# A graph stage whose edge lists are rounded to 8 columns, and whose merge and gates run by halves

## The reference

```python
h = (x_flat @ W_gat).reshape(M, HEADS, NUM_EXPERTS)       # M = 8192, 4 heads x 4 experts
src = jnp.concatenate([edge_index[0], loops]); dst = jnp.concatenate([edge_index[1], loops])
e = leaky_relu(a_src[src] + a_dst[dst], 0.2)
ee = jnp.exp(e - segment_max(e, dst)[dst])
alpha = ee / (segment_sum(ee, dst)[dst] + 1e-16)
agg = segment_sum(h[src] * alpha[:, :, None], dst).reshape(M, 16) + b_gat
scores = layernorm(agg, ln_gamma, ln_beta).reshape(M, HEADS, NUM_EXPERTS).mean(1)
topk_s, topk_i = top_k(scores, 2); w = softmax(topk_s)
# out = sum over 4 experts of gate * (gelu(x @ W1[e] + b1[e]) @ W2[e] + b2[e])
```

## Time and profile before

| what | us |
|---|---|
| median of three runs | 2720.1 |
| the profiled execution's own time | 2713.4 |
| its span, first to last instruction | 2711.6 |
| sort, stages 0 to 2, list places | 0 to 866 |
| gathers and blocks | 866 to 1567 |
| last block to first tok_end fetch | 1567 to 1579 |
| 64 fetches | 1579 to 1660 |
| merge and gates | 1660 to 1708 |
| experts of stage 3, layernorm | 1708 to 1831 |
| stages 4 to 7 | 1831 to 2712 |

### The profile page before, as it was taken

The page is one execution under the profiler, slowest core; times in us unless marked ns, Lnnn a source line. Parts: engine busy times, 40 slices in busy tenths (PEclk is TensorE's granted clock), DMA queues, the critical chain, the costliest instruction groups (busy, mean ns, idle before and its releaser), DMA issues.

```text
span 2711.6 us, 19548 instructions
## 1 busy us (share of the span) xinstructions
PE 1360.3 (50%) x6758; PEld 601.1 (22%) x6758; DVE 1406.3 (52%) x2023; ACT 634.9 (23%) x1011; POOL 813.8 (30%) x870
## 2 busy tenths in 40 slices
PE   2637421488761000000000010889977999979889
PEld 1424321322330000000000000224544222224432
DVE  7999999866634310111111114546236555566566
ACT  1301200065010000000000001543024666630043
POOL 1000000177347877777777763000000000000000
PEclk8756655599875555555555555899988999989989
DMA  9200000000134011111111100001000000000000
GB/s 394 110 1 1 0 0 0 22 14 13 27 12 69 12 20 14 20 20 14 20 20 14 20 14 5 1 1 24 0 1 4 1 1 1 1 7 0 0 1 32
DMA packets 62636, 63.00 MB, mean 23 GB/s; under 512 B 42821, under 2 KB 56533, under 8 KB 60117
## 3 DMA queue, kind: packets, MB, share of 16 engines
q1 hardware_dynamic: 36532, 52.16, 6.4%
q0 software_dynamic: 26016, 9.69, 3.5%
HBM read 21.68 MB, written 40.11 MB: 23 GB/s over the span
## 4 chain that ended last, share of the span: by engine, by line
PE 31%; POOL 28%; DVE 25%; issue 12%; ACT 1%; DMA 0%; POOLq 0%; DVEq 0%; SPq 0%; ACTq 0%
POOL rows L1766 19%; DVE keys L2029 13%; PE bank L814 9%; PE bank L505 7%; PE bank L542 7%; POOL keys L1911 5%; POOL scratch_start L1758 2%; POOL tok_end L1781 2%; PE bank L445 2%; DVE x_pair L1352 2%; PE bank L527 2%; PE bank L413 2%; DVE keys L2027 1%; PE bank L538 1%; DVE wide L451 1%
## 5 line engine op out<-in xcount | busy, mean ns | idle before, releaser
L1766 POOL DMA_INDIRECT rows<-scratch_row,idx_ring x544 | 533.2, 980 | 165.8 <-issue 165.8
L737 DVE TENSOR_TENSOR hid<-hid,bank 128x512 f32<-128x512 f32 (+1 forms) x320 | 273.0, 895 | 232.3 <-PE bank L527 231.4
L1436 PE MATMUL bank<-ident,last 128*20 128x128 f32 x3 | 0.8, 409 | 739.5 <-DVEq L1626 739.5
L2029 DVE TENSOR_TENSOR keys<-keys 128x1024 f32<-128x1024 f32 (+1 forms) x388 | 353.5, 953 | 7.3
L613 ACT ACTIVATE hid<-bank,weights_odd 128x512 f32<-128x512 f32 x448 | 281.2, 685 | 176.1 <-PE bank L505 174.4
L505 PE MATMUL bank<-wide,weights_odd 64*128 64x512 f32 x896 | 268.2, 679 | 106.0 <-ACT hid L613 105.4
L1594 DVE COPY idx_ring<-src_i 128x32 int32 (+1 forms) x17 | 3.3, 194 | 546.6 <-DMA rows<-scratch_row,idx_ring 546.4
L542 PE MATMUL bank<-hid,weights_odd 128*64 128x512 f32 x896 | 242.2, 621 | 0.5 <-DVE hid L737 0.5
L766 POOL MEMSET wide<- 128x132 f32 (+2 forms) x3 | 1.0, 333 | 748.4 <-DVEq L1053 336.8
L1911 POOL DMA_INDIRECT keys<-scratch_sorted,weights_odd x128 | 123.7, 966 | 221.4 <-DVEq L2082 179.8
L814 PE MATMUL bank<-wide,weights_even 128*128 128x512 f32 x416 | 186.4, 603 | 1.5 <-issue 1.5
(11 more groups left out here) (414 smaller groups left out, 2004.0 us busy)
## 6 DMA issues: line engine op xcount, KB each, us to landing
scratch_sums<-wide SPq DMA_DIRECT2D x12, 2048.0 KB, 35.9
rows<-scratch_row,idx_ring POOLq DMA_INDIRECT x544, 2.4
...
```

What stands on the lines that cost most here:

```text
L737: v.tensor_tensor(blocks, blocks, bank[4 + b][:, :].unsqueeze(1).broadcast_to([P, KS, 512]), ALU.mult).then_inc(S("scaled"), 1)
L1766: g.indirect_dma_start(out=rows[:, b, c, :], out_offset=None, in_=row_d[:, :], in_offset=at(idx_ring[:, b, c:c + 1])).then_inc(s_gath[b], 16)
L2029: m = v.tensor_tensor(o, p, q, op)
```

## The change

The lists' length is rounded to 8 columns (`PART`) instead of 32. Blocks that need all four parts stay in the loop; a partly filled one runs behind the loop: GpSimd gathers 8, 16 or 24 of its columns, VectorE walks all 32, and columns behind the list's end are made harmless by adding -1e30 to their `a_dst_e` (`behind_end`) and setting their `same` to 1. ScalarE and SyncE keep the old loop. The merge buffers move to another place in memory. What the merge can do without the fetched ends is done ahead; the rest runs by halves of 32 tiles: the first half and its gates ahead of the experts, the second inside VectorE's expert steps 5 to 10. ScalarE's exponentials and roots for it move among its gelus, and the next stage's layernorms of stage 3 begin at step 22 instead of 13 and follow each third step instead of each fourth.

```diff
+LATE = 5
+LN3 = [max(4 * n + 13, 3 * n + LATE + 17) for n in range(8)]
...
-        pe.wait_ge(S("s3_tok_carry"), 4)
...
-    for i in range(SPREAD_LAG, BLOCKS + LAG + 5):
+    for i in range(SPREAD_LAG, LN3[7] + 4 if st == 3 else BLOCKS + LAG + 5):
...
-        if 1 <= i - SPREAD_LAG <= 6:
-            gates_in(1 + i - SPREAD_LAG)
+        if gates_at(st, i) is not None:
+            gates_in(gates_at(st, i))
...
+        if st == 3:
+            for n in range(8):
+                if i == LN3[n] + 3:
+                    ln_back(pe, 4, n)
+            for n in range(8):
+                if i == LN3[n] + 1:
+                    ln_var(pe, 4, n)
+            for n in range(8):
+                if i == LN3[n]:
+                    ln_centre(pe, 4, n)
+        elif st != 7:
...
+    k = i - SPREAD_LAG
+    if st == 3:
+        return {1: 2, 2: 3, LATE + 7: 4, LATE + 8: 5, LATE + 9: 6, LATE + 10: 7}.get(k)
+    return 1 + k if 1 <= k <= 6 else None
...
+    for i in range(LN3[7] + 2 if st == 3 else 8 * NH + LAG + 7):
-        if i == 3:
+        if st == 3:
+            if i == SPREAD_LAG:
+                merge_exp(a, 0)
+                merge_root(a, 0)
+                gate_exp(0)
+            if i == LATE + 7:
+                merge_exp(a, 1)
+            if i == LATE + 9:
+                merge_root(a, 1)
+            if i == LATE + 11:
+                gate_exp(1)
+        if i == 3 and st != 3:
             gate_exp(0)
         if i == SPREAD_LAG:
-            gate_exp(1)
+            if st != 3:
+                gate_exp(1)
             gate_rows(0)
             gate_rows(1)
...
+        if st == 3:
+            for n in range(8):
+                if i == LN3[n] + 1:
+                    ln_root(a, 4, n)
+                if i == LN3[n]:
+                    ln_square(a, 4, n)
...
-    gate_vector(v, link, st)
+    split_gates = gate_vector(v, link, st)
+    if st == 3:
+        largest, second, shares = split_gates
+        for step in range(4):
+            merge_vector(v, link, 0, step)
+        largest(0)
+        second(0)
+        shares(0)
+    def second_half(s):
+        if LATE <= s < LATE + 4:
+            merge_vector(v, link, 1, s - LATE)
+        if s == LATE + 3:
+            largest(1)
+        if s == LATE + 4:
+            second(1)
+        if s == LATE + 5:
+            shares(1)
...
+    for s in range(LN3[7] if st == 3 else 8 * NS + 8 // KS + 1):
+        if st == 3:
+            second_half(s)
+            for n in range(8):
+                if s == LN3[n] - 5:
+                    ln_recip(v, 4, n)
+                if s == LN3[n] - 3:
+                    ln_scale(v, 4, n)
...
+def merge_exp(a, h):
+    a.wait_ge(S("s3_merge_in"), 2 + 2 * h)
+    nc.scalar.activation(wgt2[h][:, :, :, :], wgt2[h][:, :, :, :], ACT.Exp).then_inc(S("s3_merge_exp"), 1)
+def merge_root(a, h):
+    part = slice(h * HNT, (h + 1) * HNT)
+    a.wait_ge(S("s3_merge_in"), 3 + 2 * h)
+    nc.scalar.activation(sc2[:, part], sc2[:, part], ACT.Sqrt).then_inc(S("s3_merge_exp"), 1)
...
+    link(v.tensor_scalar(behind_end, col_iota, span[:, 0:1], NEG, ALU.is_ge, ALU.mult))
...
+    link(v.scalar_tensor_tensor(same[:, :], col_iota, span[:, 0:1], same[:, :], ALU.is_ge, ALU.max))
...
-    link(v.tensor_scalar(limits, list_w, float(WIN * P), None, ALU.mult))
-    link(v.memset(limits[:, 0:2], -1.0))
+    for q in range(4):
+        link(v.tensor_scalar(limits[:, q, :], list_w, float(WIN * P), float(q * PART * P), ALU.mult, ALU.add))
+    link(v.memset(limits[:, :, 0:2], -1.0))
     link(v.tensor_scalar(limits, limits, total, None, ALU.is_lt))
-    link(v.tensor_reduce(span[:, 1:2], limits, AX, ALU.add))
-    link(v.tensor_reduce(span[:, 2:4], limits.rearrange("p (i b) -> p b i", b=2), AX, ALU.add))
-    link(v.tensor_copy(blocks_i[:, 0:2], span[:, 2:4]))
-    link(v.tensor_copy(blocks_i[:, 2:3], span[:, 1:2]))
+    link(v.tensor_reduce(block_f[:, 7:8], limits.rearrange("p q w -> p (q w)"), AX, ALU.add))
+    for q, at in ((0, 0), (3, 3)):
+        link(v.tensor_reduce(block_f[:, at:at + 2], limits[:, q, :].rearrange("p (i b) -> p b i", b=2), AX, ALU.add))
+        link(v.tensor_reduce(block_f[:, at + 2:at + 3], limits[:, q, :], AX, ALU.add))
+    link(v.tensor_scalar(span[:, 0:1], block_f[:, 7:8], float(PART), None, ALU.mult))
+    link(v.scalar_tensor_tensor(block_f[:, 6:7], block_f[:, 5:6], -4.0, block_f[:, 7:8], ALU.mult, ALU.add))
+    link(v.tensor_scalar(block_f[:, 7:8], block_f[:, 6:7], float(16 * PART), None, ALU.mult))
+    link(v.tensor_tensor(block_f[:, 8:10], block_f[:, 0:2], block_f[:, 3:5], ALU.subtract))
+    link(v.tensor_scalar(block_f[:, 10:11], block_f[:, 5:6], -1.0, None, ALU.add))
+    link(v.tensor_copy(blocks_i[:, :], block_f))
...
+        window(b, b, (s_gath[b], 16 * WIN), True)
+    rest = a_dst_e[:, 2 * WIN:, :]
+    link(v.tensor_tensor(rest, rest, behind_end[:, 2 * WIN:].unsqueeze(2).broadcast_to([P, EPP - 2 * WIN, HEADS]), ALU.add))
+    full = full_blocks(v)
+    with v.Fori(1, NW // 2) as i:
+        for b in range(2):
+            with v.If(i < full[b]):
+                window(2 * i + b, b, (s_gath[b], (i + 1) * (16 * WIN)))
+    split = split_block(v)
+    for b in range(2):
+        with v.If(split[b] > 0):
+            part_rows = v.value_load(blocks_i[0:1, 7:8], min_val=16 * PART, max_val=16 * WIN)
+            g = v.value_load(blocks_i[0:1, 5:6], min_val=2, max_val=NW - 1)
...
-    v.wait_ge(S("s3_tok_end"), 16 * NT)
-    v.wait_ge(S("s3_tok_carry"), 4)
+    link(v.tensor_tensor(e_spec[:, :, :], e_spec[:, :, :], bc4(spec_off[:, :]), ALU.add))
+    link(v.tensor_tensor(m_rest, e_self[:, :, :], e_spec[:, :, :], ALU.max))
+    v.wait_ge(S("s3_tok_carry"), 4)
...
+    link(v.tensor_tensor(m_rest, m_rest, wgt[:, 1, :, :], ALU.max))
+    link(v.tensor_tensor(wgt[:, 1, :, :], wgt[:, 1, :, :], m_rest, ALU.subtract))
+    link(v.tensor_tensor(wgt[:, 2, :, :], e_self[:, :, :], m_rest, ALU.subtract))
+    link(v.tensor_tensor(wgt[:, 3, :, :], e_spec[:, :, :], m_rest, ALU.subtract))
     v.sem_inc(S("s3_merge_in"), 1)
     v.wait_ge(S("s3_merge_exp"), 1)
...
+    weigh_sums(v, link, rest_sum, tok_carry, wgt[:, 1, :, :])
     weigh_row(tmp, h_tok, wgt[:, 2, :, :])
-    link(v.tensor_tensor(agg[:, :, :], agg[:, :, :], tmp[:, :, :], ALU.add))
+    link(v.tensor_tensor(rest_sum, rest_sum, tmp, ALU.add))
     link(v.tensor_tensor(wgt[:, 3, :, :], wgt[:, 3, :, :], bc4(spec_n), ALU.mult))
     weigh_row(tmp, rep(spec_row[:, :], ROW), wgt[:, 3, :, :])
...
-    link(v.tensor_tensor(agg[:, :, :], agg[:, :, :], tmp[:, :, :], ALU.add))
...
+def merge_vector(v, link, h, step):
...
+    w, ends, rests, sums_h, other = wgt2[h], tok_end[:, part, :], rest_sum[:, part, :], agg[:, part, :], tmp[:, part, :]
...
+    if step == 0:
...
+        v.wait_ge(S(f"s3_tok_end{h}"), 16 * HNT)
+        link(v.tensor_tensor(w[:, 0, :, :], ends[:, :, ROW:ACC], has[:, part].unsqueeze(2).broadcast_to([P, HNT, HEADS]), ALU.add))
+        link(v.tensor_tensor(e_self[:, part, :], w[:, 0, :, :], m, ALU.max))
+        link(v.tensor_tensor(w[:, 1, :, :], m, e_self[:, part, :], ALU.subtract))
+        link(v.tensor_tensor(w[:, 0, :, :], w[:, 0, :, :], e_self[:, part, :], ALU.subtract))
+        v.sem_inc(S("s3_merge_in"), 1)
+    if step == 1:
+        v.wait_ge(S("s3_merge_exp"), 2 + 2 * h)
+        weigh_sums(v, link, sums_h, ends, w[:, 0, :, :])
+        weigh_sums(v, link, other, rests, w[:, 1, :, :])
+        link(v.tensor_tensor(sums_h, sums_h, other, ALU.add))
+        den = fives(sums_h)[:, :, :, GE]
+        link(v.tensor_scalar(den, den, 1e-16, None, ALU.add))
+        link(v.reciprocal(den, den))
+        link(v.tensor_tensor(A.rearrange("p t (h g) -> p t h g", g=GE), fives(sums_h)[:, :, :, 0:GE],
+                             den.unsqueeze(3).broadcast_to([P, HNT, HEADS, GE]), ALU.mult))
+        link(v.tensor_tensor(A, A, rep(W[3, "b_gat"], H16), ALU.add))
+    if step == 2:
+        link(v.tensor_reduce(mean, A, AX, ALU.add))
+        link(v.tensor_scalar(mean, mean, 1.0 / H16, None, ALU.mult))
+        link(v.tensor_tensor(A, A, mean.unsqueeze(2).broadcast_to([P, HNT, H16]), ALU.subtract))
+        link(v.tensor_tensor(T16, A, A, ALU.mult))
+        link(v.tensor_reduce(var, T16, AX, ALU.add))
+        link(v.tensor_scalar(var, var, 1.0 / H16, 1e-5, ALU.mult, ALU.add))
+        v.sem_inc(S("s3_merge_in"), 1)
+    if step == 3:
+        v.wait_ge(S("s3_merge_exp"), 3 + 2 * h)
+        link(v.reciprocal(var, var))
+        link(v.tensor_tensor(A, A, var.unsqueeze(2).broadcast_to([P, HNT, H16]), ALU.mult))
+        link(v.tensor_tensor(A, A, rep(W[3, "ln_gamma"], H16), ALU.mult))
+        link(v.tensor_tensor(A, A, rep(W[3, "ln_beta"], H16), ALU.add))
+        link(v.tensor_reduce(gates[:, part, 4:8], A.rearrange("p t (h g) -> p t g h", g=GE), AX, ALU.add))
+        scores = gt[0][:, 0:NT * 4].rearrange("p (t b e) -> p t b e", b=B, e=4)[:, 16 * h:16 * h + 16, :, :]
```

(85 more changed lines are left out.)

77 lines of the change are left out of this document (20 added, 57 removed).

## The result

The changed kernel takes 2669.0 us (median of 4 runs, 2666.7 to 2672.1) against 2719.5 before: ratio 0.9819, 95% interval 0.9802 to 0.9837. A second measurement of both gave 0.9822 (0.9803 to 0.9841). Forecast: 2676.6, faster.

What follows compares the result with a forecast made beforehand. The prediction took GpSimd's gathers, then VectorE's merge, then TensorE and VectorE alternating as the bounds. Its terms summed to -43.5 us, 2669.9 in the profile's terms and 2676.6 on the median; range 2662 to 2691, with the chances 2656 to 2698.

Steps and rivals of the forecast that it cites:

- places: In the convolution before the lists: about 10 more small VectorE instructions on the chain of waits, +2.4 us (1.5 to 4).
- steps 0 to 4: First expert steps: four copies of gate rows fewer, -1 us.
- Lists: Building the lists: two new VectorE instructions over 2048 columns hold up GpSimd's transfers, +2.0 us together (0.9 to 3.2).
- `rest`: Addition into a_dst_e after the second gather block: a GpSimd gather starting inside it waits to its end, +7.7 us.
- Short block: End of the gather loop: 8 gathers for 32, but VectorE's 24 idle turns decide its start, -14.3 us.
- Half merge: First tok_end fetch to first expert multiply: half the merge waits for only 32 fetches, -64 us (-58 to -68).
- steps 5 to 10: Expert steps carrying the second half's merge on VectorE: about 31 us for 18.7, +12.3, clock counted apart.
- Rival (d): Merge: half fetch brings nothing because the work ahead isn't done; 10 us late gives 2686; chance 0.09.
- the +4 for the clock: Expert steps 5 to 10: a few steps at a lower granted clock with TensorE about half idle, +4 us (0 to 15).
- Rival (c): Expert steps 11 to 31: TensorE stays at 1.2 GHz until the stage ends, +59 us, 2736, slower; chance 0.05.
- Rival (b): Expert loop from step 16: layernorms don't overlap, five rounds cost 4.4 more each, +22 us, 2698; chance 0.12.
- The extra round at the end: End of the stage: one layernorm round more stands behind the last multiply, +7.4 us.

Runs made afterwards that it cites:

- e_rest: Changed kernel with the addition into a_dst_e made only for the partly filled block's 32 columns, not all 7936 elements: 2657.5 us, ratio to before 0.9767.
- e_vturns: Changed kernel with only VectorE's loop over blocks ending behind the last full block, without its idle turns: 2663.7 us, ratio to before 0.9798.
- e_turns: Changed kernel with the block loops of all four engines ending behind the last block in use: 2658.7 us, ratio to before 0.9776.
- e_wait64: Changed kernel with the first half of the merge waiting for all 64 fetches: 2712.9 us, ratio to before 0.9979.
- e_noahead: Changed kernel with the moved-ahead part of the merge and ffn_spread starting only when 32 fetches are in: 2688.8 us, ratio to before 0.9883.
- e_tail: Changed kernel with the next stage's layernorm 6 in its own PSUM bank, one step behind layernorm 5, layernorm 7 at step 41: 2663.0 us, ratio 0.9794.

## Why the prediction was right

**Bounds and places.** The chain was read rightly: GpSimd, then the merge, then the alternation of TensorE and VectorE. Places held within 0.1. That steps 0 to 4 agree (-1, -0.8) is luck: they vary by more.

**Lists** were too small, +3.1 for +2.0: behind_end cost GpSimd 0.64, the maximum 1.8, and the old comparison 0.7 more than before, since a transfer now started earlier inside it. The Trainium skill, page "SBUF — State Buffer", section "Who interferes with whom", counts `tensor_scalar` among the instructions that can take the pair of ports shared with GpSimd; the trace agrees (L1585: 2048 columns in 1.29 us, a transfer 0.64 late).

**`rest`**: right in mechanism and size. The sentence of the Trainium skill, same page and section, by which a `tensor_tensor` left a transfer unharmed does not hold for these indirect gathers (8.31 us for 0.94, and back at 0.94 in e_rest).

**Short block**: right engine, right price per turn; e_vturns and e_turns show the order, VectorE first, then GpSimd.

**Half merge**: right; of the 62.2, 39.8 hang on the 32 fetches (e_wait64), and the work ahead is worth 11.7 net (e_noahead). If the two add, some 10.7 are left, the second half's work; it comes back as the +11.3 in steps 5 to 10, where VectorE is the busy engine. The 2 us of holding up that the sum took for the fetches came from no row; it was 3.6. Rival (d) falls, since 11.4 us of cover were left. ScalarE's turns were dearer in my sum (0.73) than in the trace (0.59), so the carry chain came earlier.

**Experts.** The step that failed is the +4 for the clock: it was low in steps 5 to 10 (0.83), but VectorE sets them (27.7 of 29.95 busy), and TensorE has room. Rival (c) falls: the clock was 1.00 in steps 11 to 31. Rival (b) falls: these took 63.5, with a layernorm each third step. The extra round at the end is +7.0 (forecast 7.4), from layernorms in line and the low clock that came with it (e_tail).

**The sum.** -43.5 forecast, -50.5 in the medians, 2669.0 within both ranges that the prediction gives (2662 to 2691 in its sum, 2656 to 2698 with the chances). The terms with measured sizes that hang least on the chance of the clock give +2.3 + 3.1 - 5.6 - 62.2 + 11.3 - 1.1 + 7.0 = -45.2; no run places the other 5: steps 0 to 4 and the attention vary by more than that, and the profiled runs of before differ from its others by nearly as much. The sum came as near as it did partly by luck: 5.0 forecast too much for steps 5 to 10 stand against 4.2 by which lists, short block and merge came out worse than forecast.
